# Router and node logits carried as extra columns of the value and output projections, in both layers of a two-layer tower

## The chip, the core and the metric

The kernel runs on one NeuronCore of one Trainium2 chip, one program and one launch. The core has five engines that run their own instruction streams and meet only at semaphores: TensorE (PE, matrix products, with its weight loads as PEld), VectorE (DVE), ScalarE (ACT), GpSimd (POOL) and SyncE (SP, which here only issues DMAs). The metric is the device time of one execution in microseconds, as the median of several runs. Three runs of the kernel before gave 1826.41, 1827.81 and 1836.93 us, so the median is 1827.81 us.

## What is computed

The input is 64 x 128 token ids and a table of type ids. All is float32.

```python
h = _L0_tok_ref(...)                                  # embedding + layernorm, 192 wide
h = h + _L0_attn_ref(_layernorm(h), Wq, bq, ..., Wout, bout)     # 12 heads of 16, over the 64 rows
h = h + _L0_ffn_ref(_layernorm(h), W1, b1, W2, b2, Wr, br)       # 8 experts, the best 2 of each token
h = h + _L1_attn_ref(_layernorm(h), qkv_w, ..., rel_pos_emb)     # 12 heads, over 128, relative positions
h = h + _L1_ffn_ref(_layernorm(h), weights_in, weights_out)      # tree of 21 nodes
```

Two small products in it matter here. The router of layer 0 and the tree of layer 1 both start from logits of the normalised sum:

```python
logits = xf @ Wr + br                                 # layer 0: 192 -> 8, softmax, top 2
all_logits = einsum('bsd,nd->bsn', inputs, weights_in)   # layer 1: 192 -> 21
```

where `xf` and `inputs` are `(h - mean) / sqrt(var + 1e-5)` of the sum after attention.

## The kernel before

The 8192 tokens are 64 tiles of 128. The running sum `hres` (128 partitions x 64 tiles x 192) stays in SBUF. The program is: layer 0 attention over the 64 tiles, a routing stage, 71 expert blocks of 256 tokens, layer 1 attention over the 64 tiles, and the tree with the output.

Both attention layers are software pipelines. One step of `pipeline` works on many tiles at once, each at another stage; `AGES[l]` says how many steps after its gather a tile reaches each stage. On each engine the order of work in a step is the order of the calls in `pe_steps`, `act_steps`, `dve_steps` and `pool_steps`, written by hand. Four steps make one turn of a hardware loop.

A step of layer 1 on PE is, in this order: logits of one tile (`logits_of_outputs`, L480 and L482), values (L352, L353), the turn of the attention sums (`turn_sums`, L347 and L348 into `ps_t`), queries and keys (L396), turn of the normalised input (L347 and L348 from `xn` into `ps_s`), first third of the probabilities turned (L435), output projection (L352, L353 from `oT`), relative scores (L494), the turn of the normalised output (`turn_outputs`, L347 and L348 from `zn` into `ps_s`), two halves of the attention sums (L456) with the other turns of probabilities (L435), and the scores (L382). Layer 0 has the same parts in another order, with shorter scores and no relative part.

Who waits for whom, as far as it is spoken of later:

- PE's turn of `xn` writes bank 0 of `ps_s`, which holds the scores of the step before. So it waits until DVE has read them: in layer 1 by `add_relative` (L735), in layer 0 by `subtract_maxima` (L750).
- PE's attention sums (L451, L456) write the bank `ps_v`, which holds the output projection, so they wait for DVE's `outputs` (L778). The output projection writes the same bank, so it waits until ACT has copied the values out of it (L597 in layer 0, L601 in layer 1).
- DVE's reciprocal and `on` (L720, L721) wait for the second half of the sums.
- In layer 1 the relative scores go PE, ACT (`relative_out`, L655 and L657), a store to DRAM on SP's queue (`rel_d`, L1374), and, once the store has landed, a load back in a shifted layout (`relb`, L1384). DVE's `add_relative` (L735) needs that load two steps after the store.
- POOL computes `(var + eps)^-0.5` for each layernorm (L318, L321) and issues the gathers (L336).
- The normalised output `zn` (DVE L771) is in layer 0 also stored to DRAM for the experts; in layer 1 it feeds only the logits. After `turn_outputs`, ACT copies it to `zT0` and `zT1` (L670, L671), PE multiplies it with `r_w` or `in_w`, and ACT copies the result to `logits` (L620).

## Time and profile before

| | us |
|---|---|
| median of 3 runs | 1827.81 |
| the profiled execution, device time | 1831.29 |
| its span, first to last instruction | 1829.6 |
| PE busy, whole span | 1645.3 (90%) |
| PEld busy | 1502.9 (82%) |
| DVE busy | 1314.9 (72%) |
| ACT busy | 1172.6 (64%) |
| POOL busy | 659.8 (36%) |

By time: layer 0 runs to about 486 us, routing to about 560, the experts to about 1157, layer 1 from there to about 1776, and the tree with the output to the end. The page gives shares over the whole span; a stage's own limit has to be read from the stage, so the rows below are taken from single steps of the loops.

### The profile page before, as it was taken

What the parts mean: (1) busy time and instruction counts of PE and PEld (TensorE: products, weight loads), DVE (VectorE), ACT (ScalarE), POOL (GpSimd) and SP (SyncE); (2) the same over time, 40 slices, a digit from 0 to 9 for tenths busy, and PEclk for the clock granted to TensorE, in tenths of its full rate; (3) what the DMA queues carried; (4) which work ended last, traced back from release to release, by engine and by line L of the source; (5) the groups of instructions that cost most, each with busy time, mean ns of one, the idle gap of its engine ahead of it and who ended that gap; (6) DMA issues with size and microseconds to landing.
All of it is one profiled execution on the core that took longest, in us unless ns stands there. A gap on an engine that the chain in (4) does not pass through costs nothing. (4 is left out here: it accounts for less than half of the span.)

```text
span 1829.6 us, 60456 instructions
## 1 busy us (share of the span) xinstructions
PE 1645.3 (90%) x19438; PEld 1502.9 (82%) x19438; DVE 1314.9 (72%) x2962; ACT 1172.6 (64%) x3337; POOL 659.8 (36%) x1326
## 2 busy tenths in 40 slices
PE   2999999999578799999999999579999999999966
PEld 2888888888367699999999999468888888888852
DVE  5888888887585255555555554289999999999855
ACT  2888888888374233333333333389999999999930
POOL 4455555553103133333333332334444444444200
PEclk9999999999788899999999999899999999999978
DMA  4122222222124978888888888377777777777614
GB/s 114 45 65 61 65 61 62 63 61 53 35 65 116 296 231 242 246 243 247 243 246 240 246 244 226 93 217 206 207 208 217 207 214 213 208 209 212 195 41 138
DMA packets 349282, 301.77 MB, mean 165 GB/s; under 512 B 43915, under 2 KB 314335, under 8 KB 349215
## 3 DMA queue, kind: packets, MB, share of 16 engines
q1 hardware_dynamic: 328878, 261.16, 49.6%
q0 software_dynamic: 16032, 37.51, 8.5%
q10 hardware_dynamic: 4304, 2.23, 0.5%
q8 instruction: 39, 0.64, 0.1%
q14 instruction: 29, 0.23, 0.0%
HBM read 207.77 MB, written 93.05 MB: 164 GB/s over the span
## 5 line engine op out<-in xcount | busy, mean ns | idle before, releaser
L1061 ACT ACTIVATE prob<-ps_s,b1s 128x256 f32<-128x256 f32 x426 | 179.2, 472 | 371.3 <-PE ps_s L1030 371.3
L1030 PE MATMUL ps_s<-xhi,w1hi_c 128*128 128x256 f32 x852 | 237.9, 297 | 19.8 <-DVE xhi L1160 18.1
L1030 PE MATMUL ps_s<-xhi,w1lo_c 128*128 128x256 f32 x852 | 228.5, 286 | 0.0
L964 POOL DMA_INDIRECT xs<-zn_d,idx x71 | 93.9, 1323 | 356.5 <-PE ps_t L994 354.0
L1152 DVE CAST w1hi_c<-score 128x768 fp32r<-128x768 f32 x142 | 73.3, 558 | 205.1 <-DMA score<-w1h 204.9
L1005 PE MATMUL ps_v<-probT,prob 128*128 128x192 f32 x852 | 208.3, 326 | 0.0
L1005 PE MATMUL ps_k<-probT,prob 128*128 128x192 f32 x852 | 208.1, 326 | 0.0
L396 PE MATMUL ps_q<-xT,wqk_c 128*128 128x128 f32 x1536 | 196.8, 279 | 1.1 <-ACT kT L643 0.6
L396 PEld LDWEIGHTS ps_q<-xT,wqk_c 128*128 128x128 f32 x1536 | 189.5, 196 | 1.9 <-ACT xT L664 1.0
L1030 PEld LDWEIGHTS ps_s<-xhi,w1hi_c 128*128 128x128 f32 x852 | 165.7, 195 | 22.4 <-issue 20.3
L1030 PEld LDWEIGHTS ps_s<-xhi,w1lo_c 128*128 128x128 f32 x852 | 165.8, 195 | 0.0
L583 ACT ACTIVATE prob<-score 128x768 f32<-128x768 f32 (+1 forms) x128 | 149.2, 1166 | 3.1
L1005 PEld LDWEIGHTS ps_k<-probT,prob 128*128 128x128 f32 x852 | 150.2, 190 | 0.0
L1005 PEld LDWEIGHTS ps_v<-probT,prob 128*128 128x128 f32 x852 | 146.6, 190 | 0.0
L735 DVE TENSOR_TENSOR score<-ps_s,relb 128x1536 f32<-128x1536 f32 x64 | 112.4, 1756 | 31.8 <-DMA relb<-rel_d 25.1
L456 PEld LDWEIGHTS ps_v<-vv,probT 128*64 128x64 f32 x3072 | 102.4, 139 | 30.6 <-issue 28.3
L1030 PE MATMUL ps_s<-xlo,w1hi_c 128*128 128x256 f32 x426 | 121.6, 285 | 0.0
L382 PE MATMUL ps_s<-kT,qT 32*64 32x64 f32 (+1 forms) x4608 | 113.4, 253 | 5.2 <-ACT xT L664 4.9
L456 PE MATMUL ps_v<-vv,probT 128*64 128x17 f32 x3072 | 113.3, 212 | 5.2 <-DVE hres L778 3.5
L382 PEld LDWEIGHTS ps_s<-kT,qT 32*64 32x64 f32 (+1 forms) x4608 | 91.9, 151 | 27.7 <-issue 27.5
L435 PE MATMUL ps_k<-ident,prob 128*128 128x128 f32 x704 | 112.8, 279 | 1.6 <-ACT prob L583 1.6
L321 POOL TENSOR_TENSOR rs<-veps,mhalf 128x1 f32<-128x1 f32 x192 | 108.1, 563 | 15.0
(217 smaller groups left out, 4385.1 us busy)
## 6 DMA issues: line engine op xcount, KB each, us to landing
rel_d<-rpad SPq DMA_DIRECT2D x64, 864.0 KB
relb<-rel_d SPq DMA_DIRECT2D x64, 768.0 KB, 4.7
probT<-w2h SPq DMA_DIRECT2D x71, 576.0 KB
score<-w1h SPq DMA_DIRECT2D x71, 384.0 KB
score<-w1h SPq DMA_DIRECT2D x142, 192.0 KB
ys_d<-ys SPq DMA_DIRECT2D x71, 192.0 KB
tok<-b2h SPq DMA_DIRECT2D x71, 96.0 KB
posb<-pos_w SPq DMA_DIRECT2D x128, 48.0 KB
```

The source lines that it names most:

```text
L321: pool.tensor_tensor(out[b][:], veps[b][:], mhalf[:, 0:1], ALU.pow).then_inc(S[out_ok], 1)
L382: last = pe.matmul(ps_s[t, g, a * keys:a * keys + keys], qT[q4][q, a // 2, t], kT[q4][q, a, t], start=True, stop=True)
L396: last = pe.matmul(ps_q[:, o:o + 128], qk_w[l][chunk][:, o:o + 128], (xT0, xT1)[chunk][b][:], start=(chunk == 0), stop=(chunk == 1))
L435: last = pe.transpose(ps_pt[u % 2][:, k * 128:k * 128 + 128], prob[b][:, j * 128:j * 128 + 128], ident[:])
L456: last = pe.matmul(ps_v[64 * c:64 * c + 64, j * W:(j + 1) * W], probT[b][:, j * 128 + 64 * c:j * 128 + 64 * c + 64], vv[v][:, j * W:(j + 1 ...
L583: act.activation(prob[b][:, 0:H * keys].rearrange("p (g a k) -> p g a k", g=G, a=A), score[b][:, :, :, 0:keys], ACT.Exp, scale=SCALE).then ...
L735: dve.tensor_tensor(sc, psv, relb[b][:].rearrange("p (g a) k -> p g a k", g=G), ALU.add).then_inc(S["s_rd"], 1)
L964: pool.indirect_dma_start(xs[b][:, s, :], None, zn_d, bass.IndirectOffsetOnAxis(ap=ix[b][:], axis=0)).then_inc(x_ld[b], 16)
L1005: last = pe.matmul(ps_y[s][:, 0:D], hT[b][:, c, s * 128:s * 128 + 128], w2[b][:, c, :], start=(c == 0), stop=(c == NI - 1))
L1030: last = pe.matmul(dst, w, x, start=(k == 0), stop=(k == len(terms) - 1))
L1061: last = act.activation(hT[b][:, c, :], ps_s[:, j, (c % 2) * BLK:(c % 2) * BLK + BLK], ACT.Gelu, bias=b1s[b][:, c:c + 1])
L1152: ch.step(dve.tensor_copy(w1hi[b][c][:], w1[b][c]))
```

## The change

The logits are no longer computed from the turned, normalised output. Since the projections are linear, the logits of the sum are the logits of its two parts, and the columns of the router (8) or of the tree (21) are appended to two weights that the kernel multiplies with anyway. `v_w` gets the columns themselves, so the value projection also gives the logits of the normalised input; ACT scales them back by the standard deviation (`sd`, a new power on POOL) into 21 new columns of `hres`. `o_w` gets the columns multiplied by the output projection, so the output projection also gives the logits of the attention's result, and `outputs` adds both in the same instruction as before, 200 or 213 columns wide instead of 192. The columns are centred, which takes out the mean. The scale `rsza` of each tile is kept, and applied to all tiles at once, at the start of the routing and of the tree. The product of the columns with the output projection is made on the chip, once for each layer.

```diff
+AGES = [dict(gather=0, emb=1, ln=2, xn=3, qk=4, v=4, sc=4, s=5, pt=6, o=7, on=8, ts=8, y=9, z=10),
+        dict(gather=0, emb=1, xn=2, qk=3, r=3, v=4, sc=4, s=5, pt=6, o=7, on=8, ts=8, y=8, z=9)]
+LOGITS = [E, NODES]
...
-        hres = sb("hres", [128, NT, D])
-        logits = sb("logits", [128, NT, NODES])
+        hres = sb("hres", [128, NT, D + NODES])
+        rsza = sb("rsza", [128, NT])
...
+                if deviation is not None:
+                    pool.tensor_tensor(deviation, veps[b][:], phalf[:], ALU.pow).then_inc(S["sd_ok"], 1)
...
-                    pe_project(pe, ps_v[:, 0:D], oT0[b][:], oT1[b][:], o_w[l]).then_inc(S["y_ps"], 1)
+                    pe_project(pe, ps_v[:, 0:D + LOGITS[l]], oT0[b][:], oT1[b][:], o_w[l]).then_inc(S["y_ps"], 1)
...
                     def values():
+                        act.wait_ge(S["sd_ok"], done("v"))
+                        act.activation(hres[:, bass.ds(st.tile("v"), 1), D:D + w],
+                                       ps_v[:, D:D + w].rearrange("p (o e) -> p o e", o=1), ACT.Identity, bias=0.0,
+                                       scale=sd[v][:, 0:1])
...
-                            bias = rel32s[to, half:half + 1] if l == 1 else 0.0
-                            ins = act.activation(kT[q4][to, a], of, ACT.Identity, bias=bias,
+                            ins = act.activation(kT[q4][to, a], of, ACT.Identity, bias=0.0,
...
                     def outputs():
-                        h = flat(row("y"))
-                        dve.tensor_tensor(h, ps_v[:, 0:D], h, ALU.add).then_inc(S["y_ok"], 1)
+                        w = D + LOGITS[l]
+                        h = flat(row("y", w))
+                        dve.tensor_tensor(h, ps_v[:, 0:w], h, ALU.add).then_inc(S["y_ok"], 1)
...
+                lgt = hres[:, :, D:D + NODES]
+                dve.tensor_tensor(fg, lgt, rsza[:].rearrange("p (t o) -> p t o", o=1).to_broadcast([128, NT, NODES]),
+                                  ALU.mult).then_inc(F_["scaled"], 1)
```

Gone in both layers are `turn_outputs`, `logits_of_outputs`, `turned_outputs` and `logits_out`, and in layer 1 `normalised_outputs` too. The bias of the keys in layer 1 (`rel32s`) is added once to the weights instead of in each of the four copies (L643). In layer 1 the output projection of a tile now stands in the same step as the turn of its sums (`y=8`), so the pipeline is three steps shorter there, and two in layer 0. New functions, once for each layer, ahead of layer 0 and in the routing stage:

```python
def column_sums(pe, l):      # 2 matmuls with ones
def centre(dve, l):          # 2 scalar_tensor_tensor on the new columns of v_w
def through_output(pe, l):   # 4 matmuls, wot (the transposed output weight) x the centred columns
def output_columns(act, l):  # 2 copies into the new columns of o_w
```

The loads of `r_w` and `in_w` are gone, and `wot`, `brs` and `rel_row` are loaded instead, one load more at the start and one more among the late ones. In the routing stage DVE first makes the 512 router logits (a multiplication and an addition), in the tree ACT's Gelu waits for DVE's multiplication of all 64 x 21.

The engine orders of layer 1 are redone. On PE, from the scores that end one step into the next step; a row is an instruction, with the line, the operation, the bank it writes and what it reads. Before:

```order
L382 MATMUL ps_s<-kT,qT 128x128 x12
L480 MATMUL ps_t<-win_c,zT 64x21 x2
L482 MATMUL ps_t<-win_c,zT 64x21 x2
L352 MATMUL ps_v<-wv_c,xT 128x192
L353 MATMUL ps_v<-wv_c,xT 128x192
L347 MATMUL ps_t<-ident,on 128x128
L348 MATMUL ps_t<-ident,on 64x128
```

The same place of the change:

```order
L389 MATMUL ps_s<-kT,qT 128x128 x12
L355 MATMUL ps_t<-ident,on 128x128
L356 MATMUL ps_t<-ident,on 64x128
L360 MATMUL ps_v<-wv_c,xT 128x213
L361 MATMUL ps_v<-wv_c,xT 128x213
```

The logits are gone and the turn of the sums (`on`) is the first thing of the step, ahead of the values. On DVE, from the end of the subtraction of the maxima of one step to the maxima of the next, in layer 1. Before:

```order
L853 SCALAR_TENSOR_TENSOR emb<-posb,route,emb 128x192
L771 TENSOR_SCALAR zn<-hres,mvz,rsz 128x192
...
L866 BN_AGGR mv<-st 128x2
L720 RECIPROCAL rden<-ps_v 128x12
L721 TENSOR_TENSOR on<-ps_v,rden 128x192
L735 TENSOR_TENSOR score<-ps_s,relb 128x1536
L759 TENSOR_SCALAR xn<-hres,mv,rs 128x192
L849 TENSOR_SCALAR emb<-tok,route 128x192
L742 TENSOR_REDUCE mx<-score 128x12
```

The same place of the change:

```order
L830 BN_AGGR mv<-st 128x2
L755 BN_AGGR mvz<-st6z 128x2
L679 RECIPROCAL rden<-ps_v 128x12
L813 TENSOR_SCALAR emb<-tok,route 128x192
L683 TENSOR_TENSOR on<-ps_v,rden 128x192
L817 SCALAR_TENSOR_TENSOR emb<-posb,route,emb 128x192
L721 TENSOR_SCALAR xn<-hres,mv,rs 128x192
L697 TENSOR_TENSOR score<-ps_s,relb 128x1536
L704 TENSOR_REDUCE mx<-score 128x12
```

The normalised output is gone, and the expert sum and the normalised input now stand ahead of `add_relative` (L735, now L697) instead of behind it. On ACT in layer 0, the start of a step. Before:

```order
L583 ACTIVATE prob<-score 128x768
L597 ACTIVATE vv<-ps_v 64x6x16 x4
L631 ACTIVATE qT<-ps_q 128x128
```

The same place of the change:

```order
L558 ACTIVATE prob<-score 128x768
L566 ACTIVATE hres<-ps_v,sd 128x8
L576 ACTIVATE vv<-ps_v 64x6x16 x4
L598 ACTIVATE qT<-ps_q 128x128
```

The scaled logits are copied to `hres` ahead of the values, out of the same bank.

## Rows read from the trace of the kernel before

**Rows 1.** Busy time by stretch: length, busy us (instructions) of each engine, clock, DMA, GB/s.

```profile
1189.00:1750.00 561.00, 543.83 (x7460) 485.37 (x7460) 511.45 (x908) 512.60 (x1279) 221.68 (x470) 0.99 0.74 208
```

**Rows 2.** Timeline, one step of layer 1: start us, us, instruction [idle before, releaser].

```profile
1400.61 0.36 SPq L1374 DMA_DIRECT2D rel_d<-rpad  x1
...
1400.97 0.30 PE L480 MATMUL ps_t<-win_c,zT 128*64 128x21 f32 x4
...
1401.21 1.76 DVE L735 TENSOR_TENSOR score<-ps_s,relb 128x1536 f32<-128x1536 f32 x1 [0.21 <-PE ps_s L382]
...
1401.42 0.59 PE L352 MATMUL ps_v<-wv_c,xT 128*128 128x192 f32 x2
...
1403.74 0.27 PE L347 MATMUL ps_s<-ident,xn 128*128 128x128 f32 x1
...
1403.94 0.28 ACT L631 ACTIVATE qT<-ps_q 128x128 f32<-128x128 f32 x1 [0.51 <-PE ps_q L396]
...
1405.24 0.31 SPq L1384 DMA_DIRECT2D relb<-rel_d  x1
...
1405.71 0.27 PE L347 MATMUL ps_s<-ident,zn 128*128 128x128 f32 x1
...
1406.10 0.88 PE L456 MATMUL ps_v<-vv,probT 128*64 128x17 f32 x24
...
1408.73 0.51 ACT L657 ACTIVATE rpad<-ps_t 128x396 f32<-128x396 f32 x1
...
1409.77 0.30 PE L480 MATMUL ps_t<-win_c,zT 128*64 128x21 f32 x4
```

**Rows 3.** Timeline, one step of layer 0.

```profile
339.31 0.27 PE L347 MATMUL ps_s<-ident,zn 128*128 128x128 f32 x1
...
339.87 0.52 PE L451 MATMUL ps_v<-vv,probT 128*64 128x34 f32 x12
...
341.51 0.59 PE L352 MATMUL ps_v<-wv_c,xT 128*128 128x192 f32 x2
...
342.46 1.03 ACT L597 ACTIVATE vv<-ps_v 64x96 f32<-64x96 f32 x4 [0.19 <-PE ps_v L353]
343.60 0.56 PE L352 MATMUL ps_v<-wo_c,oT 128*128 128x192 f32 x2
```

**Rows 4.** Groups by line and form: busy us, mean ns of one, idle before. Layer 0.

```profile
L321 POOL TENSOR_TENSOR rs<-veps,mhalf 128x1 f32<-128x1 f32 x58 | 32.6, 562 | 4.5
...
L643 ACT ACTIVATE kT<-ps_q,halves 64x128 f32<-64x128 f32 x59 | 21.5, 364 | 0.7
```

**Rows 5.** The same view in layer 1.

```profile
L643 ACT ACTIVATE kT<-ps_q,rel32s,halves 64x128 f32<-64x128 f32 x68 | 31.0, 455 | 0.9
...
L494 PE MATMUL ps_t<-relw,qT 128*128 128x264 f32 x68 | 20.7, 386 | 0.0
...
L353 PE MATMUL ps_v<-wv_c,xT 128*128 128x192 f32 x68 | 16.6, 326 | 0.0
```

**Rows 6.** DMA issues, whole run: count, KB, us to landing.

```profile
relb<-rel_d SPq DMA_DIRECT2D x64, 768.0 KB, 4.7
```

**Rows 7.** All instances of L735: count, durations, first and last start; idle before (us, times).

```profile
L735 DVE TENSOR_TENSOR score<-ps_s,relb x64: 1747/1758/1759, 1189.0 to 1749.6; 128x1536 f32<-128x1536 f32 x64
...
  DMA relb<-rel_d: 25.1, 27
```

**Rows 8.** Timeline of SP's queue and DVE, early in layer 1.

```profile
1239.18 0.36 SPq L1374 DMA_DIRECT2D rel_d<-rpad  x1
1245.03 0.36 SPq L1384 DMA_DIRECT2D relb<-rel_d  x1
```

**Rows 9.** Timeline of DVE, the addition that took that load.

```profile
1250.47 1.76 DVE L735 TENSOR_TENSOR score<-ps_s,relb 128x1536 f32<-128x1536 f32 x1 [1.59 <-DMA relb<-rel_d]
```

**Rows 10.** Timeline of DVE, start of the tree.

```profile
1776.02 0.86 DVE L1477 TENSOR_SCALAR relb<-logits 128x1344 f32<-128x1344 f32 x1 [2.31 <-PEq L1359]
...
1788.02 1.56 DVE L1501 TENSOR_TENSOR probT<-rpad,relb 128x1344 f32<-128x1344 f32 x1
```

More of the change, by code:

```diff
@@ L231, in tower @@
         mvz = two("mvz", [128, 2])
-        rsz = two("rsz", [128, 1])
+        sd = four("sd", [128, 1])
         vepsz = two("vepsz", [128, 1])
         zn = two("zn", [128, D])
-        zT0 = two("zT0", [128, 128])
-        zT1 = two("zT1", [D1 + 1, 128])
         mv = two("mv", [128, 2])
@@ L257, in tower @@
         oT1 = two("oT1", [128, 128])
+        wot_s = [prob[0], wo1t_s]
+        wot = [(w[:, 0:256], w[0:D1, 256:512]) for w in wot_s]
+        rel_row = wo1t_s[D1:D1 + 1, 256:256 + SLOTS * 128]
         at_lane = [kT[p][:, 0, :] for p in range(4)]
@@ L302, in tower @@
         M = [{n: [sem(f"L{l}_{n}{p}") for p in range(2)] for n in DMAS if n not in ONLY[1 - l]} for l in range(2)]
+        W_ = {n: [sem(f"W_{n}{l}") for l in range(2)] for n in ("sum", "centred", "ps", "ok")}
         dve_c = sem("dve_c")
@@ L460, in sums @@
                         last.then_inc(S["o_ps"], 1)
[L462 to L467 removed]
                 def turn_sums():
                     pe.wait_ge(S["o_sb"], done("ts"))
[L471 removed]
+                    after(pe, S["oT_sb"], before("ts"))
+                    if l == 1:
+                        after(pe, S["r_sb"], before("r"))
                     pe_transpose(pe, ps_t, on[st.two("ts")][:]).then_inc(S["oT_ps"], 1)
[L474 to L484 removed]
                 def relative():
@@ L502, in turn_inputs @@
                     pe_transpose(pe, ps_s[:, 0, :], xn[st.two("xn")][:]).then_inc(S["xT_ps"], 1)
-                def turn_outputs():
-                    pe.wait_ge(S["zn_ok"], done("zt"))
-                    bank_s()
-                    after(pe, S["zT_sb"], before("zt"))
-                    pe_transpose(pe, ps_s[:, 1, :], zn[st.two("zt")][:]).then_inc(S["zT_ps"], 1)
                 if l == 0:
@@ L550, in body @@
                         relative()
-                    if st.has("zt"):
-                        turn_outputs()
                     if st.has("o"):
@@ L937, in picks @@
                 body(PICKS - 4 + p, p)
+        def column_sums(pe, l):
+            cols = slice(D, D + LOGITS[l])
+            pe.matmul(ps_q[:, 0:LOGITS[l]], ones[:], v_w[l][0][:, cols], start=True, stop=False)
+            pe.matmul(ps_q[:, 0:LOGITS[l]], ones[:], v_w[l][1][:, cols], start=False, stop=True)\
+                .then_inc(W_["sum"][l], 1)
+        def centre(dve, l):
+            cols = slice(D, D + LOGITS[l])
+            for c, rows_ in enumerate((slice(0, 128), slice(0, D1))):
+                w = v_w[l][c][rows_, cols]
+                dve.scalar_tensor_tensor(w, ps_q[rows_, 0:LOGITS[l]], -1.0 / D, w, ALU.mult, ALU.add)\
+                    .then_inc(W_["centred"][l], 1)
+        def through_output(pe, l):
+            cols = slice(D, D + LOGITS[l])
+            pe.wait_ge(W_["centred"][l], 2)
+            for c in range(2):
+                j = slice(128 * c, 128 * c + 128)
+                pe.matmul(ps_q[:, 64 + 64 * c:64 + 64 * c + LOGITS[l]], wot[l][0][:, j], v_w[l][0][:, cols],
+                          start=True, stop=False)
+                last = pe.matmul(ps_q[:, 64 + 64 * c:64 + 64 * c + LOGITS[l]], wot[l][1][:, j], v_w[l][1][0:D1, cols],
+                                 start=False, stop=True)
+            last.then_inc(W_["ps"][l], 1)
+        def output_columns(act, l):
+            act.wait_ge(W_["ps"][l], 1)
+            for c in range(2):
+                act.activation(o_w[l][c][:, D:D + LOGITS[l]], ps_q[:, 64 + 64 * c:64 + 64 * c + LOGITS[l]], ACT.Copy)\
+                    .then_inc(W_["ok"][l], 1)
         def route_pool(pool):
@@ L1347, in _ @@
             dve.wait_ge(dve_c, 9)
+            dve.wait_ge(W_["sum"][0], 1)
+            centre(dve, 0)
             dve_steps(dve, 0)
@@ L1419, in tower @@
         fc = sb("fc", [128, NT, 32])
-        F_ = {n: sem("F_" + n) for n in ("gelu", "dve", "c_ok", "cT_ps", "cT_sb", "o_ps", "o_sb")}
+        F_ = {n: sem("F_" + n) for n in ("scaled", "gelu", "dve", "c_ok", "cT_ps", "cT_sb", "o_ps", "o_sb")}
         out_st = [sem(f"out_st{p}") for p in range(2)]
@@ L1441, in _ @@
             def _(act):
-                act.activation(fg, logits[:], ACT.Gelu).then_inc(F_["gelu"], 1)
+                act.wait_ge(F_["scaled"], 1)
+                act.activation(fg, fg, ACT.Gelu).then_inc(F_["gelu"], 1)
                 def body(m, p, k):
@@ L1553, in full_chunks, with beside @@
     return out
+def beside(w, more):
+    out = np.zeros((w.shape[0], w.shape[1] + more.shape[1]), np.float32)
+    out[:, :w.shape[1]] = w
+    out[:more.shape[0], w.shape[1]:] = more
+    return out
 def head_slots(wq, bq, wk, bk):
@@ L1581, in laid_out @@
             rel32[g, half, :, half] = rel[REL - 1]
+    relrow = np.zeros((SLOTS, G, 2, DH), np.float32)
+    relrow[2] = rel[REL - 1]
+    for g in range(G):
+        relrow[1, 2 + g % 2, odd_half(g, 2)] = rel[REL - 1]
     return {
```

227 lines of the change are left out of this document (108 added, 119 removed).

## The prediction, made before the changed kernel ran

> **What bounds the kernel now.** I began with the busy time by stretch. Layer 1 is the stage to look at: in 561 us PE is busy 543.8, DVE 511.5, ACT 512.6, and the 16 DMA engines 0.74 at 208 GB/s, at clock 0.99 [rows 1]. Three engines and the queues are all near full, so what counts is which wait ends last in one step. The timeline of a step of layer 1 shows that [rows 2]. PE starts it with the logits at 1400.97 and starts the next at 1409.77: 8.80 us, with no gap put down to another engine. DVE had to wait 0.21 us for PE's scores ahead of L735, ACT 0.51 us for the queries. So PE sets the step, and the others have slack of some tenths. In layer 0 the view of one step says the same: ACT waits 0.19 us for PE's values, PE goes from the normalised output to the second sums without a named wait [rows 3].
>
> There is a second, slower path in layer 1, which no engine's busy time shows. Relative scores leave ACT, are stored, loaded back, and are needed two steps later by L735. From the end of one L735 round to the L735 three steps later it reads: L735 itself and its semaphore 1.86; from PE's turn of `xn` (1403.74) to the end of PE's step (1409.77) 6.03; from the step's start (1400.97) to the queries on ACT (1403.94) 2.97; from there to the end of L657 (1408.73 + 0.51 = 1409.24) 5.30; then about 0.16 to the store, 4.63 from store to load (1400.61 to 1405.24) [rows 2], and 4.7 for the load to land [rows 6]. The sum is 25.65 for three steps, 8.55 a step, 0.25 below PE's 8.80. Over all 63 steps the mean is (1749.6 - 1189.0) / 63 = 8.90, and DVE waited for that load 27 times, 25.1 us in all [rows 7]. So this ring already binds at times.
>
> **The change, part by part.**
>
> *Layer 1, PE.* The logits go: 1400.97 to 1401.42, 0.45. The turn of `zn` goes: 1405.71 to 1406.10, 0.39 [rows 2]. Together 0.84 a step. Added are 21 columns in each of eight passes (two projections, two chunks, two passes of float32, as the count of records says). From 192 to 264 columns a pass grows from 326 to 386 ns [rows 5], 0.83 ns a column, so 21 x 0.83 x 8 = 0.14. PE's own step becomes 8.80 - 0.84 + 0.14 = 8.10.
>
> *Layer 1, the other engines.* in 63 steps DVE is busy 511.5 / 63 = 8.1 and ACT 512.6 / 63 = 8.1 a step [rows 1]. DVE loses one pass over 192 columns, about 0.3. ACT loses two copies of `zT` and the logits (about 0.4), gains the scaled copy (0.26, below), and its four copies of the keys get shorter by 455 - 364 ns each, 0.36 in all [rows 4, 5]. That leaves 7.8 and 7.6, under PE's 8.10, but closer to it than before. The turn of `on` moves to the head of PE's step: the logits and values that covered it (1.2 us) are gone, and if `on` is late, everything on PE behind it is late. DVE is 0.3 shorter than PE's step, and about that much ahead `on` should be ready, so I cost the move at nothing; without that cover it costs what DVE is late, step by step.
>
> *Layer 1, the ring.* The same sum: 1.86; 6.03 - 0.39 + 0.07 = 5.71; 2.97 - 0.45 + 0.07 = 2.59; ACT's 5.30 less 0.33 for the two `zT` copies (an estimate: two starts of that kind lie 0.17 apart) and 0.36 for the keys = 4.61; and 9.49 for the DMAs. It gives 24.26, 8.09 a step. That is for the DMA times of the good step. Early in layer 1 the same store took 5.85 (1239.18 to 1245.03) [rows 8] and its load was used at 1250.47 after a wait of 1.59 [rows 9]: 11.29 from store to use instead of 9.33, which makes 8.09 + 1.96 / 3 = 8.74. Which of the two it will be hangs on overlap: in the good step a load has 8.80 - 4.63 = 4.17 us before the next store is issued and needs 4.7, so they overlap by 0.5; with a step of 8.1 they overlap by 1.2. So the change moves the transfers into each other, and I take the ring between its ends, 8.40, not 8.10. Gain: (8.90 - 8.40) x 63 = 31 us, with ends at 8.15 (47) and 8.74 (10).
>
> In share of time the DMA engines are not full: 0.74 x 8.90 = 6.6 us of work a step [rows 1], so it is the latency of two transfers in a row that binds, and not the bandwidth. The Trainium skill (Trainium Kernel Development and Optimization, Key Constraints) says that DMAs issued from SP, ACT and POOL run on the same 16 engines and interleave. By that rule the 0.7 us of new overlap is paid by the load and by the store: 8.09 + 1.4 / 3 = 8.56 a step, and the whole kernel would come to 1783, inside my forecast's own range; without it the good rows alone would give the 8.10 of rival 1.
>
> *Layer 0.* From the turn of `zn` at 339.31 to the second sums at 339.87, 0.56 goes [rows 3]; eight columns in eight passes cost 8 x 0.83 x 8 = 0.05. But the scaled copy on ACT stands ahead of the four copies of the values. Those start at 342.46 and end at 343.49; PE's output projection, which writes the same bank, starts at 343.60 [rows 3]. Cover is 0.11. The new copy costs between nothing and a scaled copy of 128 columns, 0.36 [rows 4]; I take 0.26, a quarter of the 1.03, since it is as short. Then PE waits 0.26 - 0.11 + 0.02 = 0.17. Net 0.56 - 0.05 - 0.17 = 0.34 a step, over about 59 full steps 20 us; ends 0.51 (30) and 0.24 (14). POOL's new power (562 ns [rows 4]) delays the next inverse root; DVE's statistics for it now stand one instruction earlier (about 0.26), and what remains is inside DVE's wait for the output projection. If that cover is gone it costs 0.3 a step.
>
> *Ends and one-time parts.* After the last L735 at 1749.6 [rows 7] layer 1 needs until 1776.02 [rows 10], 26.4 us: its last full steps lose 0.84 each, and three short steps (the output projection's delay, turn and logits of `zn`) go; I estimate 5.5, a fifth of it, with 3 and 8 as ends. The tree gains a multiplication of 1344 elements, for which the nearest row is 1.56 [rows 10]; Gelu behind it is mostly hidden by DVE's masks; I take 2. Layer 0's end gets 3 shorter; the routing gets two passes of 512 and three small ones, 1.5 net; at the start DVE waits for the column sums, 1. Columns through the output weight are made while PE waits anyway. Sum: -5.5 + 2 - 3 + 1.5 + 1 = -4.
>
> The sum is -31 - 20 - 4 = -55 against the profiled execution's 1831.3, that is 1776. The median of the runs is 3.5 below that execution, so **1773 us**.
>
> **Rivals.**
>
> 1. *PE stays the bound, the DMAs keep their good times.* Layer 1 at 8.15, layer 0 without the wait: -47 - 30 - 4 = -81, about 1747. For it: the median load lands in 4.7 [rows 6], so good times are the common ones. Against: the overlap grows. Chance 0.15.
> 2. *The store ring takes over.* Layer 1 at 8.74 and layer 0 at its lower end: -10 - 14 - 4 = -28, about 1800. For it: the rows of the early steps, where that happened already [rows 8, 9]. Chance 0.18.
> 3. *No gain that can be measured.* `on` at the head of PE's step comes late and takes all of layer 1's gain (0.5 late each step), and POOL's 0.3 comes on top in layer 0: -20 + 18 - 4 = -6, about 1822. For it: DVE's 7.8 is close to 8.10, and L735 in front of it can slip by the load. Against: the wait for the load was 0.4 a step on average (25.1 / 63 [rows 7]), and part of it is inside the 0.3. Chance 0.08.
> 4. *Slower.* One mechanism: the load of `relb` lands so late that L735, and with it `on` and PE's first instruction, slips each step. It decides from a step of 9.3 on in layer 1 (+25 against -24 elsewhere), and 1% slower needs 9.6, so a store-to-use of 9.33 + 3 x (9.6 - 8.09) = 13.9. The longest that I saw was 11.3 [rows 8, 9]. It would give about 1850. Chance 0.03.
>
> My forecast (1760 to 1792 by itself) has 0.56.
>
> **The numbers.** Range: rival 1's middle at the low end and rival 2's far side at the high end, 1742 to 1804, which leaves out rivals 3 and 4, the lower part of rival 1 and the upper part of rival 2, together 0.2. A measurement of this kernel can tell about 1% from no change. Faster by over 1% is under 1809.5: the forecast, rivals 1 and 2 nearly whole, 0.90. Within 1%: 0.07. Slower: 0.03.
>
> **What would show it.** In layer 1: 4 matmul lines gone, L697 every 8.4 us, with waits for `relb` in most steps; stores of L1374's kind above 4.7. If L697 comes every 8.1 to 8.2, rival 1 holds; if it waits over 1 us for the load each step, rival 2. PE's turn of `on` with a wait for DVE would be rival 3's. In layer 0: PE's output projection waiting about 0.17 for ACT's `vv`, and steps 0.34 shorter. At the start of the tree about 2 us more, ahead of it 5 less. It is wrong if layer 0 does not get shorter by at least 0.2 a step, since nothing there but PE's own list is in question.

## The result, and the profile after

| | median, us | executions | ratio to before |
|---|---|---|---|
| before | 1830.04 | 11 | |
| changed | 1819.95 (1811.67 to 1831.97) | 11 | 0.994 (0.992 to 0.996) |
| changed, measured again with the experiments (e12) | 1814.96 (1809.82 to 1821.40) | 7 | 0.991 (0.988 to 0.994) |

The kernel is 0.6 to 0.9% faster, 10 to 16 us. The prediction said 55 us, 1773, and a range that ended at 1804: wrong. What came out lies in the case that had 0.07. Times are medians of the executions; in e1 one execution of four took 6548.13 us, and its time is the median of the other three.

The profiled execution of the changed kernel took 1819.95 us, its span is 1818.2. The busy times of layer 1, from the first to the last L697 (which was L735), answer to [rows 1]. Columns: stretch, its length, busy us and instructions of PE, PEld, DVE, ACT and POOL, granted clock, DMA share, GB/s.

```profile
1182.20:1731.60 549.40, 517.65 (x6902) 466.30 (x6903) 490.48 (x850) 479.31 (x1169) 260.70 (x532) 0.98 0.77 213
```

PE was busy 543.8 of 561 us before, and is busy 517.65 of 549.4 now: 94% and not 97%. Part of the work that was taken away became idle time on PE.

To see where, I cut both traces at eight instructions: DVE's first and last residual add of layer 0 (L778, now L738), the relative scores' add in layer 1 (L735, now L697; its 1st, 14th, 50th and 64th), the first instruction of the tree on DVE, and the end of the span. Both kernels were later profiled a second time, unedited (e13 and e12), and stand beside it. All in us:

| stretch | first traces: before, changed | second traces: before, changed | difference, first and second | forecast |
|---|---|---|---|---|
| start to first add of layer 0 | 66.7, 68.4 | 64.3, 64.8 | +1.6, +0.5 | +1 |
| layer 0, first to last add | 413.0, 402.1 | 412.8, 402.3 | -10.9, -10.5 | -23 |
| routing, experts, filling of layer 1 | 709.2, 711.7 | 709.2, 713.5 | +2.4, +4.2 | +1.5 |
| layer 1, first 13 steps | 114.8, 119.3 | 114.6, 118.7 | +4.4, +4.0 | |
| layer 1, the 36 steps behind | 318.6, 306.6 | 315.0, 303.0 | -12.0, -12.0 | -31 for all 63 |
| layer 1, the last 14 | 127.1, 121.8 | 124.5, 122.8 | -5.3, -1.7 | |
| drain, from the last L735/L697 to the tree | 26.5, 32.7 | 36.6, 32.2 | +6.2, -4.4 | -5.5 |
| tree and output | 53.5, 55.6 | 53.7, 54.7 | +2.1, +0.9 | +2 |
| sum | | | -11.4, -18.8 | -55 |

The rows of the changed kernel from which layer 1's lines come, out of DVE's timeline (start, length, engine, line, what it does, idle time before it and who ended that): the 1st, 14th, 50th and 64th L697.

```profile
1182.15 1.76 DVE L697 TENSOR_TENSOR score<-ps_s,relb 128x1536 f32<-128x1536 f32 x1 [4.16 <-DMA relb<-rel_d]
...
1301.42 1.76 DVE L697 TENSOR_TENSOR score<-ps_s,relb 128x1536 f32<-128x1536 f32 x1
...
1608.06 1.76 DVE L697 TENSOR_TENSOR score<-ps_s,relb 128x1536 f32<-128x1536 f32 x1 [0.55 <-DMA relb<-rel_d]
...
1729.87 1.76 DVE L697 TENSOR_TENSOR score<-ps_s,relb 128x1536 f32<-128x1536 f32 x1 [0.93 <-PE ps_s L389]
```

Four things stand out. Layer 0 got half of its gain. Layer 1's steady part gives 0.33 us a step (8.85 to 8.52, and 8.75 to 8.42). Its first 13 steps are slower than before. And the drain was 6 longer in one pair of traces, 4 shorter in the other.

**Layer 0.** The timeline of one step, cut to the instructions that touch the bank `ps_v`, with the queries and keys (L403) that PE works on between values and output projection, and on to the next first sums (two of the same line on PE are one projection):

```profile
409.45 0.54 PE L458 MATMUL ps_v<-vv,probT 128*64 128x34 f32 x12 [0.24 <-DVE hres L738]
...
410.99 0.20 DVE L679 RECIPROCAL rden<-ps_v 128x12 f32<-128x12 f32 x1
...
411.96 0.61 PE L360 MATMUL ps_v<-wv_c,xT 128*128 128x200 f32 x2
...
412.74 1.50 PE L403 MATMUL ps_q<-xT,wqk_c 128*128 128x128 f32 x12
...
413.04 0.27 ACT L566 ACTIVATE hres<-ps_v,sd 128x8 f32 x1 [0.26 <-PE ps_v L361]
413.20 1.01 ACT L576 ACTIVATE vv<-ps_v 64x96 f32<-64x96 f32 x4
...
414.32 0.58 PE L360 MATMUL ps_v<-wo_c,oT 128*128 128x200 f32 x2
...
415.39 0.37 DVE L738 TENSOR_TENSOR hres<-ps_v,hres 128x200 f32 x1 [0.33 <-PE ps_v L361]
...
416.01 0.54 PE L458 MATMUL ps_v<-vv,probT 128*64 128x34 f32 x12 [0.23 <-DVE hres L738]
```

So the bank goes round: sums to reciprocal 1.54, to the values 0.97, values to ACT's copy 1.08, copies to output projection 1.28, to DVE's add 1.07, to the next sums 0.62. That is 6.56, the distance of the adds three times out of four (the fourth is 7.07, at the loop's end). The rows of before for the same circle, beside those of [rows 3]:

```profile
342.26 1.50 PE L396 MATMUL ps_q<-xT,wqk_c 128*128 128x128 f32 x12
...
344.63 0.36 DVE L778 TENSOR_TENSOR hres<-ps_v,hres 128x192 f32 x1 [0.29 <-PE ps_v L353]
...
345.29 0.54 PE L451 MATMUL ps_v<-vv,probT 128*64 128x34 f32 x12 [0.26 <-DVE hres L778]
...
347.17 0.23 DVE L720 RECIPROCAL rden<-ps_v 128x12 f32<-128x12 f32 x1 [0.44 <-PE ps_v L451]
```

There the parts are, in the same order from the sums on, 1.88, 1.07, 0.95, 1.14, 1.03 and 0.66: 6.73. Before, the steps are 6.68 to 6.74, most of them 6.69, and 7.18 at the loop's end. So a step got 0.13 shorter, 0.11 at the loop's end.

That the parts add up to the step shows nothing by itself: any way round from an instruction to the same one a step later does. What tells is where PE waits. From the first sums to the values it works through its own list (at the loop's end it stops once). Then it waits twice. The output projection starts 1.58 behind the start of L403 (1.58 to 1.61 in each step from 150 to 425 us), and before the change 1.34 (342.26 to 343.60, the same in each step): about 0.25 of waiting for ACT's copies, which before was none. And ahead of the first sums it waits 0.23 for DVE's add, as it did before. Without the two waits the step would be 6.56 - 0.25 - 0.23 = 6.08, PE's own list. PE is busy 94% of this stretch (257.8 of 275 us), and the bank costs the rest.

**Layer 1.** The waits in 300 us of its steady part, once in the first trace of the changed kernel and once in the second (engine, line, tile, who was waited for: us in total, times, longest):

```profile
ACT qT L598 <- PE ps_q L403: 12.4, 36, 0.5
DVE rden L679 <- PE ps_v L463: 11.5, 35, 0.5
ACT probT L551 <- PE ps_k L442: 10.9, 26, 0.5
...
DVE score L697 <- DMA relb<-rel_d: 5.6, 13, 0.6
...
PE ps_v L463 <- DVE hres L738: 2.7, 11, 0.3
```

```profile
ACT qT L598 <- PE ps_q L403: 18.0, 36, 0.5
...
DVE rden L679 <- PE ps_v L463: 8.4, 36, 0.2
...
DVE score L697 <- DMA relb<-rel_d: 6.0, 15, 0.7
PE ps_v L463 <- DVE hres L738: 3.3, 14, 0.3
...
ACT probT L551 <- PE ps_k L442: 0.7, 3, 0.3
```

The load of `relb` is waited for 0.16 us a step. Over the whole layer it is 26.5 us, of which 4.2 lie ahead of the very first L697 and 12.7 in the first 13 steps. Before, it was 25.1 us in all, of which 8.5 lay ahead of the first L735 and 8.5 in the first 13 steps.

### The profile page after: what moved, and what is told of

Same layout as the page of the kernel before. It is cut to its first block and busy times, and to the rows that moved or that the text cites. A ratio compares the mean times of both kernels' runs of the same rounds, so it can differ in the third digit from the quotient of the medians.

```text
span 1818.2 us, 57166 instructions
## 1 busy us (share of the span) xinstructions
PE 1612.0 (89%) x18182; PEld 1466.3 (81%) x18182; DVE 1299.9 (71%) x2904; ACT 1120.7 (62%) x3085; POOL 732.0 (40%) x1455
## 5 line engine op out<-in xcount | busy, mean ns | idle before, releaser
L959 POOL DMA_INDIRECT xs<-zn_d,idx x71 | 85.5, 1205 | 361.4 <-PE ps_t L995 359.0
L403 PE MATMUL ps_q<-xT,wqk_c 128*128 128x128 f32 x1536 | 197.6, 280 | 0.5 <-ACT xT L630 0.5
L403 PEld LDWEIGHTS ps_q<-xT,wqk_c 128*128 128x128 f32 x1536 | 195.5, 197 | 1.0 <-ACT xT L630 1.0
L609 ACT ACTIVATE kT<-ps_q,halves 128x128 f32<-128x128 f32 (+1 forms) x512 | 172.9, 364 | 4.9
L697 DVE TENSOR_TENSOR score<-ps_s,relb 128x1536 f32<-128x1536 f32 x64 | 112.5, 1758 | 32.3 <-DMA relb<-rel_d 26.5
L463 PEld LDWEIGHTS ps_v<-vv,probT 128*64 128x64 f32 x3072 | 105.0, 141 | 36.7 <-issue 31.0
L551 ACT ACTIVATE probT<-ps_k 128x512 f32<-128x512 f32 (+1 forms) x192 | 107.2, 559 | 40.1 <-PE ps_k L442 34.9
L463 PE MATMUL ps_v<-vv,probT 128*64 128x17 f32 x3072 | 115.8, 214 | 14.3 <-DVE hres L738 10.4
```

The source lines that it names most:

```text
L403: last = pe.matmul(ps_q[:, o:o + 128], qk_w[l][chunk][:, o:o + 128], (xT0, xT1)[chunk][b][:], start=(chunk == 0), stop=(chunk == 1))
L463: last = pe.matmul(ps_v[64 * c:64 * c + 64, j * W:(j + 1) * W], probT[b][:, j * 128 + 64 * c:j * 128 + 64 * c + 64], vv[v][:, j * W:(j + 1 ...
L551: act.activation(probT[b][:, u * w:(u + 1) * w], ps_pt[u % 2][:, 0:w], ACT.Copy)\
L609: ins = act.activation(kT[q4][to, a], of, ACT.Identity, bias=0.0, scale=halves[(hi if of is not third else to), half:half + 1])
L697: dve.tensor_tensor(sc, psv, relb[b][:].rearrange("p (g a) k -> p g a k", g=G), ALU.add).then_inc(S["s_rd"], 1)
L959: pool.indirect_dma_start(xs[b][:, s, :], None, zn_d, bass.IndirectOffsetOnAxis(ap=ix[b][:], axis=0)).then_inc(x_ld[b], 16)
```

## The experiments

### e1: layer 0 without the scaled copy

```diff
-                        act.activation(hres[:, bass.ds(st.tile("v"), 1), D:D + w],
+                        if l == 1:
+                            act.activation(hres[:, bass.ds(st.tile("v"), 1), D:D + w],
```

> Layer 0 without the scaled copy of the router logits on ACT (the eight columns are computed but stay in the bank; they are zero in the sum, so the routing is another one). My theory A: layer 0's step of 6.56 us is one chain through the bank ps_v (values, ACT's copies, output projection, DVE's add, second sums, reciprocal, `on`, values again), and the scaled copy stands on it with its start (0.16) and some 0.1 of pickup. Then a step is 6.56 - 0.16 to 0.27 and layer 0 gets 9 to 15 us shorter, nothing else moves. The rival, POOL's added powers on the path or PE's own list as the bound: the step stays at 6.56 and the time too.

Measured: 1804.98, ratio 0.985 (0.983 to 0.987). Layer 0's step is 6.30 (6.81 at the loop's end), and layer 0 takes 387.9 and not 402.1 us. The rows of one step:

```profile
396.31 0.61 PE L360 MATMUL ps_v<-wv_c,xT 128*128 128x200 f32 x2
...
397.09 1.50 PE L403 MATMUL ps_q<-xT,wqk_c 128*128 128x128 f32 x12
397.29 1.03 ACT L577 ACTIVATE vv<-ps_v 64x96 f32<-64x96 f32 x4 [0.15 <-PE ps_v L361]
398.43 0.57 PE L360 MATMUL ps_v<-wo_c,oT 128*128 128x200 f32 x2
```

The copy costs 0.26 a step, which is the size that the prediction gave it. But there is no cover. Without the copy, PE's output projection starts 1.34 behind L403, as before the change, and 0.11 behind the end of ACT's work (398.32, 398.43). In the changed kernel, where PE does wait for ACT, it starts 0.11 behind it too (414.21, 414.32). So 0.11 is the time of handing over, not slack: before the change PE's list and ACT's copies reached the projection at the same moment, and the copy put ahead of them delays it in full. POOL still does its extra power here, and the step is shorter all the same: it is not on the chain.

### e2: the output projection in banks of its own

```diff
+        y_at = (ps_t, ps_s[:, 1])
...
-                    after(pe, S["v_sb"], done("v"))
-                    after(pe, S["o_sb"], before("o"))
-                    after(pe, S["y_ok"], before("y"))
-                    pe_project(pe, ps_v[:, 0:D + LOGITS[l]], oT0[b][:], oT1[b][:], o_w[l])
+                    if l == 1:
+                        bank_s()
+                        after(pe, S["y_ok"], before("y"))
+                    else:
+                        after(pe, S["y_ok"], before("y"))
+                        after(pe, S["oT_sb"], done("y"))
+                    pe_project(pe, y_at[l][:, 0:D + LOGITS[l]], oT0[b][:], oT1[b][:], o_w[l])
```

The edit is shown without its switch for each layer, which is on in both. The first sums and the values no longer wait for `y_ok`; the scores of layer 1 and the turn of `on` in layer 0 do. That turn also moved behind the second sums, and no run separates the move from the bank.

> The output projection leaves the values' bank: layer 0 writes it into ps_t (and turns `on` behind the second sums), layer 1 into bank 1 of ps_s. Nothing is left out. Theory A says that in both layers the bank chain through DVE's add sets the step (6.56 in layer 0; in layer 1 the 8.55 from L697 over L738, both sums, L679 to L697). Broken up, layer 0 falls to PE's own list, about 6.2 to 6.3, and layer 1 from a steady 8.50 to PE's 8.23 or to the ring of the stores, at most 8.4: 17 and 8 us less. Rival 1 (layer 1 is bound by the store and load of the relative scores): layer 0 gains the same, layer 1 stays at 8.50. Rival 2 (PE is full anyway): neither gains more than 0.05 a step.

Measured: 1767.90, ratio 0.966 (0.964 to 0.969). Layer 0 takes 370.6 us, 31.5 less than the changed kernel; the add comes every 6.06 to 6.14, and 6.27 at the loop's end. Layer 1's 36 steady steps are 8.29 each, against 8.52 and 8.42. PE's rows in a step of layer 0:

```profile
399.31 1.50 PE L407 MATMUL ps_q<-xT,wqk_c 128*128 128x128 f32 x12
400.65 0.50 PE L362 MATMUL ps_t<-wo_c,oT 128*128 128x200 f32 x2
```

The projection is back at 1.34, and PE waits for no add ahead of the sums. The step is about the 6.08 that is left of the changed kernel's when its two waits are taken off. So these waits at the bank are what layer 0 takes beyond PE's own list. In layer 1 the bank costs 0.13 to 0.23 a step. PE's list in a step of layer 1, with nothing in its way:

```profile
1510.53 0.33 PE L357 MATMUL ps_t<-ident,on 128*128 128x128 f32 x1
...
1512.86 0.27 PE L357 MATMUL ps_s<-ident,xn 128*128 128x128 f32 x1
...
1514.24 0.83 PE L500 MATMUL ps_t<-relw,qT 128*128 128x264 f32 x4
...
1515.00 0.88 PE L477 MATMUL ps_v<-vv,probT 128*64 128x17 f32 x24
...
1518.68 0.33 PE L357 MATMUL ps_t<-ident,on 128*128 128x128 f32 x1
```

It is 8.15 long, and no steady step is shorter. The prediction had 8.10. In the changed kernel the sums start 0.84 behind L484's first record (1705.79, 1706.63) and not 0.76, and the best full step is 8.23.

The Trainium skill (Perfetto Trace Analysis, Optimizing Tensor Performance, Matmuls) says that independent groups of matmuls should rotate through different PSUM banks, so that the copying out of one overlaps the matmuls of the next. The trace agrees with 0.48 us a step in layer 0 (6.56 against 6.08).

### e5 and e9: half of the store

```diff
-                        sp.dma_start(heads[:, :, 0:LPAD + REL], rpad[b][:])
+                        nh = H if isinstance(t, int) and t < 2 else H // 2
+                        sp.dma_start(heads[:, 0:nh, 0:LPAD + REL], rpad[b][:, 0:nh])
```

> From the third tile of layer 1 on only the first six of the twelve heads' relative scores are stored (the other six keep what an earlier tile left, so the scores of those heads are not those of the reference); the load is whole. Theory C: in layer 1's first 14 steps the ring of store and load sets the pace (127.8 us instead of 14 x 8.53 = 119.5, with waits of L697 for `relb`), while later it is the bank chain. Then those 14 steps fall to about 120 and the steady ones stay at 8.50 to 8.54: 6 to 9 us less. Rival, the ring binds throughout: the steady steps fall too, by 0.2 or more, 20 us in all. Second rival, the first steps are slow for another reason: no change.

Measured: 1796.03, ratio 0.983 (0.978 to 0.987). The waits of L697, over all of layer 1, in e5 and in the changed kernel:

```profile
L697 DVE TENSOR_TENSOR score<-ps_s,relb x64: 1742/1750/1758, 1183.3 to 1712.6; 128x1536 f32<-128x1536 f32 x64
...
  DMA relb<-rel_d: 5.2, 2
```

```profile
L697 DVE TENSOR_TENSOR score<-ps_s,relb x64: 1750/1758/1760, 1182.2 to 1729.9; 128x1536 f32<-128x1536 f32 x64
...
  DMA relb<-rel_d: 26.5, 25
```

Of the 5.2 us 4.1 lie ahead of the very first L697. The first 13 steps take 109.9 us and not 119.3; the steady ones are 8.41, the same as in the second trace of the changed kernel; the last 14 steps take 116.6 (121.8 and 122.8). So the ring of store and load binds at both ends of layer 1, and in the middle not to speak of. At the beginning SP's queue reads, in the changed kernel:

```profile
1193.52 0.36 SPq L1404 DMA_DIRECT2D relb<-rel_d  x1
1197.35 0.36 SPq L1394 DMA_DIRECT2D rel_d<-rpad  x1
1203.57 0.36 SPq L1404 DMA_DIRECT2D relb<-rel_d  x1
1205.48 0.36 SPq L1394 DMA_DIRECT2D rel_d<-rpad  x1
1211.85 0.36 SPq L1404 DMA_DIRECT2D relb<-rel_d  x1
```

The second store is issued 1.9 us behind a load, and the load that waits for it comes 6.4 later, against the 4.63 of [rows 2]. That is rival 2's result, but only for 13 steps. Its mechanism, the overlap, is not shown: the first store here is issued 3.8 behind its load, as stores in the middle are too, whose loads come 4.6 later, and here it takes 6.2. What makes the transfers of these steps long stays open.

> e2 (the output projection in banks of its own) with e5's half store (from the third tile of layer 1 on six of twelve heads are stored; the output is not the reference's). If theory A is whole, then behind the bank chain stands the ring of store and load, and behind that PE's own list: e2's steady step of 8.29 falls to PE's own 8.08 to 8.15, and the first 14 steps fall by 8 us or more: 1767.9 - 36 x 0.15 - 8 = about 1754. Rival: DVE's own list (about 8.3 busy) is what bounds e2, and the steady step stays within 0.05 of 8.29.

Measured: 1760.01, ratio 0.963 (0.960 to 0.966). The first 13 steps take 109.5 us, in e2 118.5, as expected (the ring again). The steady step did not: 8.42, where e2 has 8.29 and 8.08 to 8.15 was expected. Neither theory had it. The waits for `relb` are gone in these 300 us, and another transfer is waited for in their place, the gathered rows of the experts' output:

```profile
DVE emb L829 <- DMA posb<-ys_d,idxb: 19.7, 28, 1.3
ACT qT L614 <- PE ps_q L407: 19.6, 36, 0.7
PE ps_t L357 <- DVE on L699: 7.3, 16, 0.9
```

Why POOL's gather is later when SP's store is smaller I did not follow up. It shows that behind the bank and the store's ring layer 1 has a third wait; whether PE's own 8.15 is in reach stays open. And PE's first instruction waits here for DVE's `on`, 16 times in 36 steps: rival 3's mechanism, which the changed kernel hardly has.

### e6 and e7: two small things on layer 1's chain

```diff
-                    expert_sum(2)
                     outputs()
+                    expert_sum(2)
```

> Layer 1: DVE's add of the output projection (L738) stands one instruction earlier, ahead of the experts' sum (L821, 0.34 us) and not behind it; nothing else differs. Theory A for layer 1: the chain L697, L704, L821, L738, first sums, second sums, L679, L697 sets the step (8.55). Then a steady step gets up to 0.34 shorter, less the wait of L738 for PE's output projection, which ended 0.17 us after L821 started: 8.53 to about 8.3, 10 us over 46 steps. Rival, PE's own list plus small waits on ACT is the bound: the steady step moves by less than 0.05.

Measured: 1810.08, ratio 0.989 (0.985 to 0.993), a steady step of 8.38.

```diff
-                        act.activation(hres[:, bass.ds(st.tile("v"), 1), D:D + w],
+                        if l == 0:
+                            act.activation(hres[:, bass.ds(st.tile("v"), 1), D:D + w],
```

> Layer 1 without ACT's scaled copy of the 21 node logits (they stay zero in the sum, so the output lacks the residual's part). Theory A: in layer 1 the copy isn't on the chain, because the output projection comes 0.7 us after the values' copy ends; the steady step stays at 8.50 to 8.54, and the time within 3 us. Rival, ACT's waits (0.5 us for the turned probabilities' PE work) come from its being full: each step gains up to the copy's 0.16, 7 to 10 us.

Measured: 1812.40, ratio 0.991 (0.988 to 0.994), a steady step of 8.39, but 123.5 us for the first 13. Against 8.52 they would be gains of 0.14 and 0.13, and e7 would refute theory A. Against the second trace of the changed kernel, 8.42, they are 0.04 and 0.03. With one trace of the changed kernel I would have read both wrongly. So e7's rival, 0.16 a step, did not come, and neither did e6's 0.2: DVE's add one instruction earlier hardly shortens the step, so that theory A, the chain over this add, is not the whole of layer 1.

The long start of e7 has another cause than the ring alone, the clock that is granted to PE. Its step from 1278.9 took 11.74 us. The view of stretches there:

```profile
1281.00:1293.00 12.00, 12.00 (x108) 10.46 (x107) 8.19 (x15) 7.40 (x15) 4.28 (x9) 0.57 0.65 174
```

PE is busy all the time, at about half the clock. The changed kernel has the same on a smaller scale: L697 waits 2.64 for `relb` at 1227.66, the granted clock from 1229 to 1234 is 0.66, and the step takes 9.51, with no wait for `relb` at its end. Of the time that the first 13 steps lost, some is therefore the clock's.

### e12: the changed kernel again

> The changed kernel once more, nothing edited. e11 has the same instructions up to step 67 of layer 1, and its steady step there is 8.42 us with 4 waits of ACT for the turned probabilities in 36 steps, against 8.52 with 26 such waits in the changed kernel's trace. Theory D: these are two gaits of one program, which differ from execution to execution; this run shows either 8.42 or 8.52 with the same sign in ACT's waits, a drain of 32 to 33 us at a clock of 0.5, and layer 0 at 6.56 again. Rival: the gait belongs to the program (its code is placed otherwise), and this run shows 8.52 again.

Measured: 8.42 a steady step, ACT's waits for `ps_k` 0.7 us in 3 steps (rows above), layer 0 at 6.56, drain 32.2. Layer 1 has two gaits. Four traces (the changed kernel, e1, e3, e4) have 8.52 to 8.53 and 26 to 32 such waits in 300 us; five (e5, e6, e7, e11 and e12) have 8.38 to 8.42 and at most 4. The program's layer 1 is the same in the changed kernel, e1, e11 and e12, as far as the steady part goes. The kernel before has two step times as well, 8.85 and 8.75. What sets the gait is open; e1, e3 and e4 were measured together, and so were e5, e6 and e7, so it may go with the measurement as well as with the execution. Its worth is 0.1 a step, 6 us if it held for all 63 steps.

### e3, e4, e11 and e8: the drain

```diff
-on=8, ts=8, y=8, z=9)]
+on=8, ts=8, y=9, z=10)]
```

> Layer 1 with y=9 and z=10 in AGES instead of 8 and 9, as before the change, all else as after it. Theory B: the 6 us that layer 1's drain lost come from the output projection's waiting for `on`'s turn and ACT's copy in the same step (0.5 to 0.6 a step), which leaves PE idle and its clock at 1.2 GHz. With y a step later PE has work while ACT copies; the drain has one step more, but the clock holds longer: drain of 28 to 33 us, the steady steps the same 8.50. Rival: one more step of drain costs 7 us more, 39 in all, since the clock falls anyway.

Measured: 1816.21, ratio 0.992 (0.990 to 0.994); a drain of 33.0 us with the clock at 0.58, and steady steps of 8.53. Neither a gain nor the rival's 7 us: the age of `y` hardly matters for the drain.

```diff
+                def keep_busy(k, first):
+                    if l == 1 and isinstance(st.n, int) and st.n >= first:
+                        bank_s()
+                        for _ in range(k):
+                            pe.matmul(ps_s[:, 2, 0:256], ident[:], wo1t_s[:, 0:256], start=True, stop=True)
```

> Extra matmuls of 256 columns, whose output nobody reads, in layer 1's last steps (two ahead of the first sums from step 64 on, three ahead of the first turn of the probabilities, one ahead of the output projection, two behind the second sums), so that PE isn't idle while it waits. Theory B, the drain lost its time to the clock: the granted clock of 1700 to 1760 stays near 1.0 and the drain goes from 32.7 us to 25 to 28, though the extra matmuls are in it. Rival, the drain is a chain of ACT and DVE with short matmuls in it: the clock may rise, but the drain stays at 32 or gets longer by the 0.4 that each extra matmul takes.

Measured: 1815.48, ratio 0.992 (0.990 to 0.995); a drain of 29.6 us, where 25 to 28 was expected. The clock rose to 0.94, but the extra matmuls waited for DVE's L697 themselves (3.17 us once), so they stood in the wrong place.

In e11 and e8 they stand elsewhere:

```diff
                     if st.has("pt"):
+                        keep_busy(4, 68, ps_v)
                         turn_probs(0)
                     if st.has("y"):
+                        keep_busy(1, 70, ps_v)
                         out_project()
...
+                if st.has("o"):
+                    keep_busy(2, 68, ps_s)
```

> The changed kernel with e8's extra matmuls in layer 1's last steps and nothing else. Theory B: the granted clock of the drain stays near 1.0 and the drain falls from 32.7 us to 26 or 27 (e8 against e2 gave 6.8 less), the time to about 1809. Rival, the drain of the changed kernel hangs on the residual add between output projection and first sums, which e8 didn't have: 29 to 31 as in e4.

Measured: 1806.57, ratio 0.991 (0.988 to 0.994). The drains of the changed kernel and of e11, by the view of stretches (columns as above):

```profile
1729.90:1762.50 32.60, 21.30 (x192) 16.57 (x190) 10.42 (x21) 7.30 (x16) 2.97 (x8) 0.58 0.00 1
```

```profile
1723.10:1749.30 26.20, 19.69 (x224) 16.20 (x224) 10.44 (x21) 7.54 (x16) 2.96 (x8) 0.98 0.01 1
```

With more matmuls in it, the drain is 6.4 us shorter, and PE's busy time less. (The medians don't show it: e11 and e12 both have a ratio of 0.991, with intervals of 0.3% either way.) In the changed kernel the clock falls from 2.4 to 1.2 GHz at about 1735, and the 24 matmuls of L463 go from 0.88 to 1.47:

```profile
1733.95 0.88 PE L463 MATMUL ps_v<-vv,probT 128*64 128x17 f32 x24 [1.66 <-DVE hres L738]
...
1743.58 1.47 PE L463 MATMUL ps_v<-vv,probT 128*64 128x17 f32 x24 [0.67 <-DVE hres L738]
...
1749.54 1.08 PE L360 MATMUL ps_v<-wo_c,oT 128*128 128x213 f32 x2 [0.58 <-ACT oT L589]
```

> Both: the output projection in banks of its own (as in e2) and extra matmuls in layer 1's last steps, now placed where PE waits for ACT only (four ahead of the first turn of the probabilities and two at the step's end from step 68 on, one ahead of the output projection from step 70 on), and never behind DVE's L697. Theory B: the granted clock of the drain stays above 0.9 and the drain falls from e2's 30.6 to about 26, so 1763. Rival, the drain is ACT's and DVE's chain: 30 or more, 1768.

Measured: 1760.01, ratio 0.964 (0.960 to 0.968), the fastest whole kernel here. Drain 23.8 at clock 0.98, against e2's 30.6 at 0.54. Theory B holds twice, with 6.4 and 6.8 us.

The Trainium skill (TensorE: Matmul & The Clock Gate, Part 1: The HAM clock gate) says that the slow clock is the default, and that activity of the array releases it. The traces agree for the drain. There the engine is never idle for long: in the changed kernel's drain its waits are 0.5 to 0.8 us and two of 1.6 to 1.7, the clock falls behind the first of these two and stays low to the end of the drain and beyond; with the gaps filled it stays high. In e7's stretch above the clock was low with PE busy all the time, which that sentence does not explain.

### e13 and e10: the kernel before

> The kernel before once more, nothing edited. Theory E: the drain of layer 1 comes at either clock in the kernel before too; in its first trace it was 26.5 us with the clock back at 1.0 after 1753, in e10 (another bank, same drain) 36.2 us at 0.5. Then this trace shows a drain of 26 to 27, or of 35 to 37 with the clock at 0.5, and the executions with the lower mean clock are the longer ones. Rival: e10's own change made its drain long, and this one shows 26 to 27 with all executions alike.

Measured: 1830.88, ratio 1.001 (0.998 to 1.004). Its drain, and that of the first trace of before:

```profile
1740.50:1777.00 36.50, 30.22 (x264) 23.93 (x264) 12.71 (x30) 10.33 (x38) 3.71 (x10) 0.56 0.00 1
```

```profile
1749.60:1776.00 26.40, 21.05 (x274) 17.07 (x274) 12.68 (x30) 10.77 (x39) 3.71 (x10) 0.89 0.01 2
```

The same program, 36.5 and 26.4. So the drain before the change comes at either clock too. (In the first trace the granted clock was 0.50 from 1745 to 1753, at the end of layer 1's full steps, and 1.00 from 1756 on.) In this measurement the executions of before with a mean clock up to 0.957 took 1836.7 to 1841.7, those from 0.965 on 1824.8 to 1828.3. Like against like, at the low clock, the change takes 4.4 us off the drain (36.6 to 32.2), or 4.0 against e10's.

> The kernel before the change, with layer 1's output projection in bank 2 of ps_s; layer 0 as it was. Theory A says that before the change PE itself was full in layer 1 (8.80 to 8.85 a step), so that the bank chain had slack there and became the bound only when the change shortened PE's list. Then nothing moves: 8.85 a step, and a time within 4 us of before. Rival: the bank chain bound the kernel before as well; its steps fall by 0.15 or more, 7 us or more.

```diff
+        y_at = (ps_v, ps_s[:, 2])
...
-                    pe_project(pe, ps_v[:, 0:D], oT0[b][:], oT1[b][:], o_w[l])
+                    pe_project(pe, y_at[l][:, 0:D], oT0[b][:], oT1[b][:], o_w[l])
```

Measured: 1830.50, ratio 1.001 (0.998 to 1.004). The steady step is 8.75, the same as in e13, the drain 36.2. Before the change the bank chain was not the bound in layer 1. That PE's own list was is argued, from PE's rows without a named wait in [rows 2]. The change shortened the list under the chain.

## Why the prediction was wrong, point by point

- **Layer 0, the step that failed.** "Net 0.56 - 0.05 - 0.17 = 0.34 a step": it was 0.13 (6.69 to 6.56, and 6.73 to 6.56 in the step of [rows 3]). Two terms were mis-sized. The removed turn and logits shorten the way from the first sums to the values by 0.44 and not by 0.56 (1.88 and 1.07 to 1.54 and 0.97). And the scaled copy costs its full 0.26 (e1), since "cover is 0.11" took the handing over from ACT to PE for slack. 0.44 - 0.26 - 0.05 is 0.13. In the first 54 steps that made 6 us (the first two got longer), and the last nine, in which the pipeline runs empty, gave 4.7, where 3 was forecast: 10.5 to 10.9 in all, and not 23. The row for the copy was in [rows 3]; what I did not ask was whether PE's list reached the output projection at the very moment at which ACT's copies allowed it. It did, and so there was nothing to hide the copy behind.
- **POOL's cover.** Right: its one power more in a step costs nothing (e1, e2).
- **Layer 1, PE's own step of 8.10.** Nearly right: 8.15 in e2.
- **Layer 1, the step of 8.40.** Measured 8.52 and 8.42: the size was right by luck, the reason was not. I had taken a middle between PE's 8.10 and a ring at 8.74. In the steady part L697 waits 0.16 a step for the ring, but without these waits (e5) the step is 8.41, so they cost next to nothing; the bank `ps_v` costs 0.13 to 0.23 (e2). What holds the step at 8.3 there is open. I had also taken 25.1 / 63 = 0.4 a step for the wait for the load before the change; 8.5 of the 25.1 lay ahead of the first L735, which leaves 0.26.
- **Layer 1, "(8.90 - 8.40) x 63", the other step that failed.** The 8.90 was a mean with the slow last 14 steps in it (9.1 each), and the 8.40 was that of a steady step. Like against like it is 8.85 to 8.52, or 8.75 to 8.42: 0.33, and it holds for 36 steps, 12 us. The first 13 steps lost 4 instead of gaining 4: the waits for `relb` in them grew from 8.5 to 12.7 us, the ring takes over (with half of the store, e5, they take 109.9 and not 119.3), and the lower clock behind such a wait adds to it. That was rival 2, in one part of the layer, though its overlap of store and load is not shown to be the reason.
- **The turn of `on` at the head of PE's step, costed at nothing.** Right: PE's wait for it stands in no steady step, and once in the last 14 (1.4 us). Rival 3 named the size of the result (1822) by a mechanism that isn't there.
- **The drain, -5.5.** At one and the same clock it is -4.4. In the first pair of traces it is +6.2, with one drain mostly at 2.4 GHz (0.89) and the other mostly at 1.2 (0.58). I had no term for the clock in it.
- **Start, routing, tree.** +1, +1.5 and +2 were +0.5 to 1.6, +2.4 to 4.2 (with the experts, which I did not take apart), and +0.9 to 2.1.

Of the 55 us, 12 were missing in layer 0. In layer 1, at the forecast's 0.5 a step, 10 to 11 were missing in the first 13 steps, where 4 were lost and not 6.5 gained, 6 in the 36 steady ones, and 2 to 5 in the last 14. The test that I had named, that layer 0 must get at least 0.2 shorter a step, failed.

## What to carry to other kernels

Before costing an instruction that is removed or put in, follow every buffer that several engines take turns on, from one write to the same write a step later, and ask at each hand-over who comes first: does the next engine stand and wait, or does it arrive later by its own list? The sum of the parts is the step in any case and tells nothing. The time from an engine's end to its successor's start (0.11 here) is no slack. An engine that is busy 94% can still wait in each step. Whether a buffer binds is shown by moving one member of the circle away: in layer 0 and in layer 1 of the changed kernel that shortened the step, in layer 1 of the kernel before it did nothing. Giving the output projection a bank of its own (with the move of the turn in layer 0) was worth some 50 us here, three to five times the change itself. And a difference below 1% between two traces should be read only after the same program has been traced twice.

## What I had not expected of the hardware

- PE's clock decided the drain of this pipeline: 24 matmuls of L463 in 1.47 and not 0.88 us, and 6.4 us of 32.6 in all (e11), with waits of 0.5 to 1.7 us between its instructions. In a full step it shows as well (11.74 us in e7, with PE busy throughout). The same program has it in one execution and not in another (26.4 and 36.5 us).
- The handing over from ACT's last copy to PE's next matmul takes 0.11 us where PE waits for it (414.21 to 414.32).
- One program keeps, over 36 steps, one of two step times 0.1 apart (8.42 and 8.52; before 8.75 and 8.85). Its cause stays open, as does why a smaller store made the gathers late in e9.
